# Flamingo block on one core: the long score products between the transposed blocks of an attention step

## The reference, cut to what matters

```python
x = x + tanh(g_xattn) * attention(layernorm(x), ctx, ctx, mask)       # 8 x 224 x 2048, 32 heads, 8 key/value heads, 750 context rows
x = x + tanh(g_ffn) * ffn(layernorm(x), ...)                          # the change touches nothing of this part

def attention(q, k, v, mask):          # q (8,224,8,4,64), k and v (8,750,8,64)
    scores = einsum('bsgrd,btgd->bgrst', q, k) / 8 + mask
    probs = softmax(scores)
    return einsum('bgrst,btgd->bsgrd', probs, v)
```

## Time and profile before

| | us |
|---|---|
| median of three runs | 1172.99 (1172.75 to 1173.55) |
| span of the profiled execution | 1170.6 |
| PE busy, share of the span | 1132.7, 97% |
| PE weight loads | 905.0, 77% |
| DVE busy | 947.1, 81% |
| ACT busy | 912.7, 78% |
| POOL busy | 905.0, 77% |

### The profile page before, as it was taken

One profiled execution on the slowest core, in us unless ns is written; L12 is line 12 of the kernel. 1 busy time (PEld: TensorE's weight loads), 2 busy tenths in 40 slices (PEclk: granted clock), 3 DMA queues, 4 the chain that ended last, 5 costly groups with the idle time before them and its releaser, 6 DMA issues.

```text
span 1170.6 us, 35223 instructions
## 1 busy us (share of the span) xinstructions
PE 1132.7 (97%) x14435; PEld 905.0 (77%) x14692; DVE 947.1 (81%) x2261; ACT 912.7 (78%) x1226; POOL 905.0 (77%) x824
## 2 busy tenths in 40 slices
PE   5999999999999999999999999999999999999998
PEld 3888888888888888888888888888887655555554
DVE  6988888888888888888888888888874899676776
ACT  5898898888898898899899988988882443655454
POOL 6999999999999999999999999999992110333424
PEclk9999999999999999999999999999999999999999
DMA  9421231133114212411331132122116600002214
GB/s 346 141 69 48 60 114 43 54 75 106 41 43 106 81 49 53 122 42 52 73 111 42 42 69 55 48 53 57 43 64 199 239 2 1 1 36 109 108 78 175
DMA packets 61599, 95.09 MB, mean 81 GB/s; under 512 B 35329, under 2 KB 44545, under 8 KB 57602
## 3 DMA queue, kind: packets, MB, share of 16 engines
q1 hardware_dynamic: 60722, 91.79, 25.7%
q10 hardware_dynamic: 720, 1.05, 0.3%
HBM read 71.75 MB, written 20.97 MB: 79 GB/s over the span
## 4 chain that ended last, share of the span: by engine, by line
PE 73%; POOL 20%; issue 2%; DVE 2%; DMA 1%; ACT 1%; DVEq 0%; SPq 0%; POOLq 0%
POOL arena L600 14%; PE psum L974 12%; PE psum L1027 12%; PE psum L951 11%; PE psum L981 6%; PE psum L962 6%; PE psum L1004 5%; PE psum L998 5%; PE psum L999 5%; PE psum L1108 3%; POOL arena L567 2%; PE psum L1014 2%; PE psum L929 2%; POOL arena L620 1%; PE psum L1077 1%
## 5 line engine op out<-in xcount | busy, mean ns | idle before, releaser
L600 POOL TENSOR_TENSOR arena<-arena 128x768 bf16<-128x768 f32 x448 | 651.6, 1469 | 39.6 <-ACT arena L761 37.1
L1360 DVE CUSTOM_DVE_ANT_0 arena<-psum,arena 128x750 f32<-128x750 f32 x448 | 420.5, 939 | 126.6 <-PE psum L962 121.0
L761 ACT ACTIVATE arena<-psum 128x768 f32<-128x768 f32 x448 | 362.3, 809 | 89.0 <-PE psum L981 88.9
L765 ACT ACTIVATE arena<-arena,neg_max 128x750 f32<-128x750 f32 x448 | 410.9, 917 | 3.8 <-DVE neg_max L1360 3.7
L974 PE MATMUL psum<-ident,arena 128*128 128x128 f32 x1792 | 268.3, 272 | 0.0
L998 PEld LDWEIGHTS psum<-arena 128*128 128x128 bf16 (+1 forms) x2688 | 194.7, 98 | 57.5
L951 PE MATMUL psum<-arena 128*128 128x512 bf16 x674 | 221.5, 383 | 15.0 <-DVE arena L1257 0.8
L999 PE MATMUL psum<-arena 128*128 128x64 bf16 (+1 forms) x2688 | 222.0, 193 | 0.0
L998 PE MATMUL psum<-arena 128*128 128x65 bf16 (+1 forms) x2688 | 221.7, 194 | 0.0
L999 PEld LDWEIGHTS psum<-arena 128*128 128x128 bf16 (+1 forms) x2688 | 178.5, 98 | 53.2
L974 PEld LDWEIGHTS psum<-ident,arena 128*128 128x128 f32 x1792 | 206.3, 140 | 4.3
(11 more groups left out here) (172 smaller groups left out, 1307.8 us busy)
## 6 DMA issues: line engine op xcount, KB each, us to landing
arena<-in_k_t SPq DMA_DIRECT2D x128, 187.5 KB, 3.2
arena<-in_v_rows SPq DMA_DIRECT2D x64, 192.0 KB, 2.5
out<-arena SPq DMA_DIRECT2D x10, 1024.0 KB, 3.9
arena<-in_x_top SPq DMA_DIRECT2D x8, 1024.0 KB, 5.3
arena<-in_x_rest SPq DMA_DIRECT2D x8, 768.0 KB, 4.6
spill<-arena SPq DMA_DIRECT2D x96, 64.0 KB, 2.2
arena<-spill SPq DMA_DIRECT2D x6, 1024.0 KB, 9.7
arena<-in_w_t SPq DMA_DIRECT2D x4, 1024.0 KB, 19.5
```

Source lines behind the costliest of these rows:

```text
L600: pool.tensor_tensor(p_lo[:, n % RING, :], p_sb[:, n % RING, :], high(p_sb[:, n % RING, :]), ALU.subtract).then_inc(p_split, 1)
L761: act.activation(p_sb[:, n % RING, :], flat_ps[:, turned_at(n):turned_at(n) + CW], ACT.Copy).then_inc(evac_a, 1)
L765: act.activation(s_sb[:, n % RING, 0:CTX], s_sb[:, n % RING, 0:CTX], ACT.Exp, bias=neg_max[:, n % 4, :], scale=-1.0).then_inc(exped, 1)
L1360: dve.tensor_tensor_reduce(s_sb[:, n % RING, 0:CTX], flat_ps[:, score_at(n):score_at(n) + CTX], mask_sb[:, max(n % UNITS - REP + 1, 0), :] ...
```

## The change

In a step, the six transpositions and the two long products stood apart: six blocks, then the product with the upper halves of the keys, then the one with the lower halves. Now three blocks come first, then the product with the upper halves, the fourth block, the product with the lower halves, then the last two blocks. `turned`, the semaphore that ACT's eviction waits for, is still set by the sixth block. The waits go with their instructions: the long product's waits stand before the fourth block, the wait for the eviction one unit back before the fifth. `score_main` is divided into its waits (`score_waits`) and its products (`score_half`), `turn_main` and `turn_mid` become `turn_block`, and `turn_and_score` sets the order. No instruction is added or removed, and nothing changes on another engine.

```diff
+            def turn_and_score(n, s):
+
+                turns, scores = 0 <= n < NU, 0 <= s < NU
+                own, shared = (tuple(main_chunks(n)), tuple(mid_chunks(n))) if turns else ((), ())
+                if turns:
+                    pe.wait_ge(exped, n + 1)
...
+                    if n >= 2:
+                        evac_wait(pe, n - 2)
+                    turn_block(n, own[0])
+                    turn_block(n, own[1])
+                    turn_block(n, own[2])
+                if scores:
+                    score_waits(s)
+                    score_half(s, True, False)
+                if turns:
+                    turn_block(n, own[3])
+                if scores:
+                    score_half(s, True, True)
+                if turns:
+                    if n >= 1:
+                        evac_wait(pe, n - 1)
+                    turn_block(n, shared[0])
+                    turn_block(n, shared[1]).then_inc(turned, 1)
...
-                if 0 <= k + 2 < NU:
-                    turn_main(k + 2)
-                    turn_mid(k + 2)
-                if 0 <= k + 5 < NU:
-                    score_main(k + 5)
+                turn_and_score(k + 2, k + 5)
```

More of the change, by code:

```diff
@@ L930, in turn_rows, with score_waits @@
                 mm.then_inc(q_turned, 1)
-            def score_main(n):
+            def score_waits(n):
                 g, m = n // UNITS, n % UNITS
                 pair = g // 2
-                half, turn = turned_slot(n)
+                half = turned_slot(n)[0]
                 if m == 0:
@@ L947, in score_main, with score_half @@
                     pe.wait_ge(maxed, n - 1)
[L948 to L954, removed]
+            def score_half(n, main, low):
                 g = n // UNITS
@@ L956, in score_mid, with turn_block @@
                 half, turn = turned_slot(n)
+                cols = score_cols(n, main)
+                kk = k_lo[:, g % 2, cols] if low else high(k_raw[:, g % 2, cols])
+                return pe.matmul(flat_ps[:, score_at(n) + cols.start:score_at(n) + cols.stop], q_t[:, g // 2 % 2, half, turn, :], kk,
+                                 start=not low, stop=low)
+            def turn_block(n, c):
+                at = turned_at(n) + c * 128
+                return pe.transpose(flat_ps[:, at:at + 128], s_sb[:, n % RING, c * 128:(c + 1) * 128], ident[:, :])
@@ new lines, in turn_and_score @@
+            def turn_and_score(n, s):
[3 more added lines that the diff above has]
+                    pe.wait_ge(exped, n + 1)
+                    if n == 0:
+                        pe.wait_ge(pads_zero, 1)
+                    if n >= 2:
[15 more added lines that the diff above has]
+                    turn_block(n, shared[1]).then_inc(turned, 1)
@@ L957, in score_mid @@
+            def score_mid(n):
                 if n >= 1:
                     pe.wait_ge(maxed, n)
[L959 to L982, removed]
+                score_half(n, False, False)
@@ L984, in value @@
+                score_half(n, False, True).then_inc(scored, 1)
             def value(n):
```

## The result

| | before | after |
|---|---|---|
| median, us | 1173.34 (1172.75 to 1173.63, 8 runs) | 1176.47 (1175.99 to 1177.15, 8 runs) |
| ratio to before, 95% interval | | 1.0028 [1.0017, 1.0038] |
| span of the profiled execution | 1170.6 | 1174.7 |

The change makes the kernel 3.1 us slower, 0.3%. The measured time lies inside the forecast range, 2.4 us above the forecast value of 1174.1. Of these, 0.35 are the median before, 1172.99 in the three runs ahead of the prediction and 1173.34 in all eight.

What follows compares the result with a forecast made beforehand. The prediction took PE, busy 97% of the span, as the bound. Closer blocks (-0.9) and waits for POOL (+2.0) gave +1.1 us on the median of 1172.99, about 1174.1 us, range 1170.0 to 1178.3.

Steps and rivals of the forecast that it cites:

- Nothing to win on PE, no cost at the junctions: On PE in an attention step: no wait to remove, and none of the four changed transposition/product junctions costs anything.
- rival 3: At PE's blocks: f32 weight loads set their spacing, so two loads a step vanish under long products, 47 us, 1127; chance 0.04.
- The term of -0.9 us from closer blocks: On PE: transpositions shortly behind a product take 108.5 ns, not 109.2, about 2 ns a step, 0.9 us less over 445.
- `turned` 0.44 later, and the eviction and POOL's split with it: Sixth block set 0.44 us later in the step; ACT's eviction slides by it, POOL's split too where POOL waited for ACT.
- The fifth block's wait: PE's wait for the eviction one unit back: worst slack falls from 0.12 to 0.01 us, cost zero.
- Rival 1: At the fifth block behind a normalization: PE loses 0.1 us in one or two units a window, 6 to 12 us; chance 0.20.
- Five pairs at 0.31 and two at 0.44: PE waiting for POOL in seven layernorm-factor windows: 0.31 us in 3, 27, 35, 43, 51; 0.44 in 11, 19; upper value 2.4.
- some hundredths absorbed: Where ACT started its eviction behind the signal, part of 0.44 is absorbed: 0.06 less in each of seven windows, giving 2.0 us.
- no second payment follows in the same run: In a run of POOL's work: after one wait PE has slid as well, so it pays only once.
- The sign named beforehand: PE's waits at L1014 for POOL grow from 5 to about 15 places, 3 us in all, in seven clusters.
- Start and end zero: First blocks late at the start, three steps without scores at the end: both cost zero, start bounds -0.4 and +0.5 us.
- Sum: Whole kernel: -0.9 us on PE plus 2.0 us of waits for POOL, +1.1 us.

## Why the prediction was right, and where it was off

- *Nothing to win on PE, no cost at the junctions.* Held: with both products ahead of the blocks and with one between, the time follows the signal, not the alternation. The f32 blocks stayed 0.11 apart beside long products; rival 3 is out.
- *The term of -0.9 us from closer blocks.* Wrong in sign, because it looked at a part of the step alone. The blocks next to a product are indeed 108.4 ns apart and not 109.2; the product before the fourth block takes about 1.5 ns more (up to 230 ns, 227 before) and the second one 1.6 less. From the first block to the first value product a step is 0.8 ns shorter, 1096.9 against 1097.7 in the mean of over 300 steps. That is less than half of the 2 ns expected. But the twelve value products with the upper halves take 363.6 ns instead of 361.1, which the prediction left out, so a whole step is 1.4 ns longer, 0.6 us over the kernel. The same 2.5 to 2.8 ns come with the blocks in one run behind the products, and with one product between, so they follow neither the alternation nor the delay of the signal. Why they come, and why the longer step vanishes when the lower-half products stand between the short ones, is left open.
- *`turned` 0.44 later, and the eviction and POOL's split with it.* Held: POOL's split 0.45 later in window 27.
- *The fifth block's wait.* Held at zero; the slack of 0.01 did not become a stall, as behind window 2 no step grew beyond the 1.4 ns but those of the pairs and the last. PE's wait for ACT at a transposition is still a single one. Rival 1, at its named place, did not happen.
- *Five pairs at 0.31 and two at 0.44.* Measured 0.30 to 0.31 five times and 0.44 and 0.43: 2.4 us, of which the longer step is 0.02 a pair; the waits are 2.3. The step that was off is the one after it, "some hundredths absorbed", 0.06 a pair, which took 2.4 down to 2.0: 0.02 a pair is missing at most. That "no second payment follows in the same run" is wrong as it stands: five pairs pay 0.21 at a load with 0.26 to spare and 0.08 more at the one with 0.18. The sum is right even so, since the last and tightest load sets it. The sign named beforehand, waits at about 15 places, 3 us in all, was 9 places and 3.0 us at the loads.
- *Start and end zero.* Window 63 costs 0.09, at the last unit, here and in five more of the seven runs with both long products ahead of the signal (the seventh has longer steps throughout). The start was not predictable to better than a microsecond.
- *Sum.* Predicted -0.9 + 2.0 = +1.1; shown +0.46 (the 46 other windows) + 2.4 + 0.09 = +2.95, against 3.1 in the medians. The mechanism was right; what missed are the sign of the smallest term, 1.5 us of the difference, and the rounding down of the largest, 0.3. With them the outcome was a clear slowdown instead of one just below what can be told, and it got a chance of 0.29.

## What to carry to other kernels

An instruction that moves behind others on a full engine costs that engine nothing and can still cost the kernel: look for the semaphore that it sets, follow it to the engine with the least to spare, and compare the shift with the slack at every place where that engine's result is waited for. Average shares hide this; POOL at 77% of the span had 0.18 us left in five windows out of 64, and the price was the shift less that slack, with 0.05 more for the release. Where PE waits for such an engine in a few windows only, moving its deferrable work out of them is worth more than reordering PE: 2.0 us here for a few lines.

## What the runs showed of the hardware

- A block transposition in f32 (128x128) holds PE for 0.108 us. Its weight load is hidden under a product of 238 columns (0.10 us), but not under one of 65 columns (0.03): there, in the run with the lower halves last, the first block takes 0.14, about 30 ns more.
- 512 columns read from the upper halves of f32 words take 0.227 to 0.230 us, and 512 packed bf16 columns 0.215 to 0.217; in the step above (404.61 to 404.84, and 404.95 to 405.16) both stand between the same kind of block. The product with the upper halves is also the one that starts the sum in PSUM, and no run parts the two.
- A weight load that waited for POOL's split went 0.05 us behind its end (401.95 to 402.00, 407.62 to 407.67).
- The trace's first record of TensorE's clock stands at 16.9 to 17.8 us in six of the eleven profiles and at 21.3 to 23.0 in five. The start of POOL's split of the keys of window 2, which waits for their load in all but one of them, varies from 37.43 to 38.73.
